# Graph attention on one core: first edges of nodes found from one gathered chunk row per group of seven nodes

## What is computed

```
h = relu(layernorm(x));  x = x + gat(h, [src, dst], edge_attr)
h = (h @ W_node.T)              # 4 heads x 32
e = (edge_attr @ W_edge.T)
att = sum([h[src], h[tgt], e] * a);  att = leaky(att, 0.2)
m = max(segment_max(att, tgt), 0);  ex = exp(att - m[tgt])
denom = segment_sum(ex, tgt) + (num_edges - deg) * exp(-m)
h_prime = segment_sum(ex / denom[tgt] * h[src], tgt)
```

## Time and profile before

| | us |
|---|---|
| median of 3 runs | 4975.68 |
| their range | 4975.63 to 4978.6 |
| profiled execution | 4962.95 |
| its span in the trace | 4955.9 |
| busy: POOL / DVE / ACT / PE | 3712.2 / 2412.0 / 1368.3 / 777.3 |

### The profile page before, as it was taken

How to read it: one execution, slowest core, us unless ns; L and a number is a source line. 1 busy time by engine, 2 the same in 40 slices (tenths; PEclk the granted TensorE clock), 3 DMA queues, 4 the chain that set the end, 5 groups by cost and what they waited for, 6 DMA issues and landing times.

```text
span 4955.9 us, 14358 instructions
## 1 busy us (share of the span) xinstructions
PE 777.3 (16%) x1453; PEld 390.6 (8%) x1453; DVE 2412.0 (49%) x2384; ACT 1368.3 (28%) x1021; POOL 3712.2 (75%) x3530
## 2 busy tenths in 40 slices
PE   5321111111111111111111111111111111111100
PEld 3310000000000000000000000000000000000000
DVE  7337454545445454454544545445454454544543
ACT  7013232222322222222222322223222232222320
POOL 6667777777777777777777777777777777777766
PEclk9555555555555555555555555555555555555555
DMA  7234444343443434434344343433434434343353
GB/s 250 90 132 119 140 123 128 114 137 114 126 125 114 137 114 128 123 115 137 114 127 123 114 136 114 129 121 115 137 114 128 122 115 136 114 131 120 116 170 104
DMA packets 171831, 627.97 MB, mean 127 GB/s; under 512 B 72897, under 2 KB 73666, under 8 KB 155426
## 3 DMA queue, kind: packets, MB, share of 16 engines
q0 software_dynamic: 115936, 252.37, 21.0%
q1 hardware_dynamic: 55874, 375.39, 20.1%
HBM read 382.66 MB, written 244.86 MB: 127 GB/s over the span
## 4 chain that ended last, share of the span: by engine, by line
POOL 70%; issue 24%; another core or an unknown queue 2%; ACT 2%; DVE 1%; PE 0%; DMA 0%; POOLq 0%; ACTq 0%; DVEq 0%; SPq 0%
POOL slots L308 69%; ACT pen L375 1%; DVE pen L482 0%; PE ae L792 0%; DVE slots L496 0%; ACT big L392 0%; ACT slots L391 0%; POOL tdst_scratch L311 0%; ACT R L421 0%; PE wexp L785 0%; DMA state_scratch<-R 0%; DVE V L636 0%; DVE slots L501 0%; DMA cols<-in_cols_dram 0%
## 5 line engine op out<-in xcount | busy, mean ns | idle before, releaser
L308 POOL DMA_INDIRECT slots<-rows_scratch,idx x3224 | 3421.5, 1061 | 1066.5 <-issue 1066.5
L803 PE MATMUL ae<-eab,w_att 128*128 128x416 f32 x992 | 650.6, 829 | 3796.2 <-DMA eab<-in_ea_dram 2539.1
L603 DVE TENSOR_TENSOR z<-slots,big 128x104 f32<-128x104 f32 (+1 forms) x125 | 43.1, 345 | 2116.3 <-DMA slots<-rows_scratch,idx 1887.3
L636 DVE TENSOR_TENSOR_SCAN V<-A,V 128x1848 f32<-128x1848 f32 x248 | 993.7, 4007 | 35.4 <-issue 4.8
L421 ACT COPY R<-V 128x1716 f32<-128x1716 f32 x248 | 777.8, 3136 | 339.1 <-DVE V L636 196.7
L417 ACT ACTIVATE A<-D 128x1848 f32<-128x1848 f32 x246 | 419.7, 1706 | 744.7 <-DVE V L636 410.3
L803 PEld LDWEIGHTS ae<-eab,w_att 128*128 128x128 f32 x992 | 296.0, 313 | 4150.4 <-issue 3384.4
L626 DVE TENSOR_TENSOR V<-slots,wexp 128x1716 f32<-128x1716 f32 x125 | 404.8, 3239 | 22.4 <-issue 21.0
L626 DVE TENSOR_TENSOR V<-slots,extra 128x1716 f32<-128x1716 f32 x123 | 398.2, 3237 | 22.0 <-issue 16.3
L438 ACT ACTIVATE wexp<-D 128x104 f32<-128x104 f32 x62 | 16.2, 261 | 1092.5 <-DVEq L621 628.8
L438 ACT ACTIVATE extra<-D 128x104 f32<-128x104 f32 x61 | 15.9, 261 | 1063.2 <-DVEq L621 631.2
(11 more groups left out here) (168 smaller groups left out, 602.3 us busy)
## 6 DMA issues: line engine op xcount, KB each, us to landing
state_scratch<-R SPq DMA_DIRECT2D x123, 1768.0 KB
eab<-in_ea_dram SPq DMA_DIRECT2D x126, 832.0 KB
slots<-rows_scratch,idx POOLq DMA_INDIRECT x3224
rows_scratch<-slots SPq DMA_DIRECT2D x14, 476.0 KB
tdst_scratch<-eab SPq DMA_DIRECT2D x4, 1612.0 KB
big<-tdst_scratch SPq DMA_DIRECT2D x8, 806.0 KB
big<-in_x_t_dram SPq DMA_DIRECT2D x14, 448.0 KB, 4.3
big<-in_x_dram SPq DMA_DIRECT2D x7, 896.0 KB
```

Of the source, the lines that this page charges most:

```text
L308: pool.indirect_dma_start(buf, None, table, bass.IndirectOffsetOnAxis(ap=index, axis=0)).then_inc(done, 16)
L636: nc.vector.tensor_tensor_scan(V[:, v, :], a_all, V[:, v, :], 0.0, ALU.mult, ALU.add).then_inc(scanned, 1)
L803: last = mm(ps_ae[k][:, 0:KB * Q], w_att[:, a * P:(a + 1) * P], eab[:, k, a * KB * Q:(a + 1) * KB * Q], start=a == 0, stop=a == 3)
```

## The change

The list is now cut into `CL` = 1024 chunks of `CE` = 403 edges. Only the first node of each group of seven has its chunk looked up (14 counts on ACT over 1024 values, 14 gathers, all into buffers of their own). All seven nodes of the group are counted in that one row: groups 2, 3, 6, 7, 8, 11, 12 and 13 (`BY_ACT`) by ACT with a Sign over 403 values, the other six by DVE. One node more, the first of the next group, is counted early by DVE where a batch ends.

A node whose first edge lies beyond that chunk gets it in another way. For each chunk (eight on a partition) and each of the six nodes that follow the last target of the chunk before, DVE counts the values below the node in the chunk (`chunk_heads`, 48 counts over 403 values of `dst_s`). The results are scattered in eight scatters as rows of six to `heads_scratch`, which is filled with a large negative number beforehand, and loaded back; `latest_heads` takes for each node the maximum of what the chunk heads up to six nodes before it say, and `positions` the maximum of that and the count. The positions are made in three batches of groups, 0 to 3, 4 to 8 and 9 to 13.

The load of `dst` moves ahead of the 14 loads of `x_t`. The making of `pen_a` (before: lines 540 to 543) moves behind the last projection copy. SP gets the fill of `heads_scratch`, their load behind the fills of `tdst_scratch`, and a small DMA that brings each partition the count of the next one's first node.

```diff
-CL = 512
-CE = P * T // CL
+CHUNKS = 8
+CL = P * CHUNKS
+CE = T // CHUNKS
...
-COUNTS = (0, 2, 4, 7, 12, 20, 29, 38, 47, 56, 65, 74, 83, 92, 99)
+FOLLOW = NG - 1
+LOOKED_UP = (0, 2, 4, 7, 10, 14)
+BATCHES = ((0, 4), (4, 9), (9, 14))
+BY_ACT = (2, 3, 6, 7, 8, 11, 12, 13)
...
+            sp.dma_start(heads_d[0:NP, :].rearrange("(p w) j -> p (w j)", p=P), fill[:, 0:W * FOLLOW]).then_inc(heads_filled, 16)
             for k in range(H):
                 sp.wait_ge(centre_done, 8 + k)
                 sp.dma_start(td_rows[:, k * T:(k + 1) * T], fill).then_inc(tdst_filled, 16)
+            sp.wait_ge(heads_put, 16 * CHUNKS)
+            sp.dma_start(heads, heads_d[0:NP, :].rearrange("(p w) j -> p (w j)", p=P)).then_inc(heads_loaded, 16)
+            sp.wait_ge(put_ready, 1)
+            sp.dma_start(cnt[0:P - 1, W:W + 1], cnt[1:P, 0:1]).then_inc(next_count, 16)
...
-            for k in range(W + 1):
-                if k in COUNTS:
-                    pool.wait_ge(chunk_ready, COUNTS.index(k) + 1)
-                if k >= RING:
-                    pool.wait_ge(chunk_used, k - RING + 1)
-                gather(ring[:, k % RING, :], dst16[:, :], chunk_i[:, k:k + 1], chunk_dma[k % RING])
+            for g in range(STEPS):
+                if g in LOOKED_UP:
+                    pool.wait_ge(chunk_ready, LOOKED_UP.index(g) + 1)
+                gather(ring[:, g, :], dst16[:, :], chunk_i[:, g:g + 1], chunk_dma[g])
+            pool.wait_ge(heads_filled, 16)
+            pool.wait_ge(heads_ready, 1)
+            for c in range(CHUNKS):
+                scatter(heads_d[:, :], head_i[:, c:c + 1], head_pos[:, c * FOLLOW:(c + 1) * FOLLOW], heads_put)
             pool.wait_ge(tdst_filled, 64)
             for g in range(STEPS):
-                pool.wait_ge(put_ready, 1 if g < STEPS - 1 else 2)
+                pool.wait_ge(put_ready, sum(g >= a for a, b in BATCHES))
...
+            def count_group(g):
+                act.wait_ge(chunk_dma[g], 16)
+                for n in range(NG):
+                    k = g * NG + n
+                    nc.scalar.activation(junk_c[n], ring[:, g, :], ACT.Sign, bias=half_n[:, k:k + 1], scale=-1.0, accum_out=sgn_w[:, k:k + 1])
+                act.drain()
+                nc.scalar.activation(within[:, g * NG:(g + 1) * NG], sgn_w[:, g * NG:(g + 1) * NG], ACT.Copy, bias=CE / 2.0, scale=0.5).then_inc(act_counted, 1)
...
+            def chunk_heads():
...
+                for j in range(FOLLOW):
+                    dve.drain()
+                    for c in range(CHUNKS):
+                        k = c * FOLLOW + j
+                        nc.vector.tensor_scalar(junk_v[c], dst_s[:, c * CE:(c + 1) * CE], bound[:, k:k + 1], None, ALU.is_lt, ALU.add,
+                                                accum_out=below[:, k:k + 1])
...
+            def latest_heads():
...
+                dve.wait_ge(heads_loaded, 16)
+                for j in range(1, NG):
+                    nc.vector.tensor_tensor(to[:, :, j:NG], to[:, :, j:NG], of[:, :, 1:NG + 1 - j, j - 1], ALU.max)
+                    dve.drain()
...
+                dve.wait_ge(act_counted, sum(g < gb for g in BY_ACT))
...
+                nc.vector.tensor_tensor(cnt[:, a:b], cnt[:, a:b], head_max[:, a:b], ALU.max)
...
+            chunk_heads()
+            count_groups(0, 4, True)
+            variance(0)
+            variance(1)
+            latest_heads()
+            inverse_deviation()
+            positions(0)
+            for g in range(3):
+                project_copy(g)
+            count_groups(4, 9, True)
+            project_copy(3)
+            dve.drain()
+            positions(1)
+            project_copy(4)
+            project_copy(5)
+            count_groups(9, 14, False)
+            project_copy(6)
+            dve.drain()
+            positions(2)
             nc.vector.tensor_scalar(rest[:, :], deg[:, :], -1.0, float(E), ALU.mult, ALU.add).then_inc(rest_ready, 1)
-            for g in range(2, STEPS):
+            for g in range(7, STEPS):
                 project_copy(g)
+            nc.vector.tensor_tensor(pen_a[:, 1:T], dst_s[:, 1:T], dst_s[:, 0:T - 1], ALU.is_equal)
+            nc.vector.memset(pen_a[:, 0:1], 0.0)
+            dve.drain()
+            nc.vector.tensor_scalar(pen_a[:, :], pen_a[:, :], 2.0 * BIG, -BIG, ALU.mult, ALU.add).then_inc(pen_a_done, 1)
```

More of the change, by code:

```diff
@@ L3 @@
 from contextlib import ExitStack
+import itertools
 P = 128
@@ L32, with graph_attention_kernel @@
 ITERS = PAIRS // UP
-RING = 8
 PIECES = 8
 PT = T // PIECES
-COUNTS = (0, 2, 4, 7, 12, 20, 29, 38, 47, 56, 65, 74, 83, 92, 99)
+FOLLOW = NG - 1
+LOOKED_UP = (0, 2, 4, 7, 10, 14)
+BATCHES = ((0, 4), (4, 9), (9, 14))
+BY_ACT = (2, 3, 6, 7, 8, 11, 12, 13)
 Q = 32
 GW = P + Q
-def graph_attention_kernel(nc, x, x_t, src, dstf, dst16, lasts, ends, first, ea, w_node, w_node_t, a_blk, we2,
+def graph_attention_kernel(nc, x, x_t, src, dstf, dst16, lasts, chunk_ends, ends, first, ea, w_node, w_node_t, a_blk, we2,
                            ident_c, centre_c, cols_c, out):
@@ L372, in count_chunks @@
             def count_chunks(m):
-                a, b = COUNTS[m], COUNTS[m + 1]
-                for k in range(a, b):
-                    nc.scalar.activation(junk_a[k % 9], last_b[:, :], ACT.Sign, bias=half_n[:, k:k + 1], scale=-1.0, accum_out=sgn[:, k:k + 1])
+                a, b = LOOKED_UP[m], LOOKED_UP[m + 1]
+                for g in range(a, b):
+                    nc.scalar.activation(junk_a[g % 4], last_b[:, :], ACT.Sign, bias=half_n[:, g * NG:g * NG + 1], scale=-1.0, accum_out=sgn[:, g:g + 1])
                 act.drain()
@@ new lines, in count_groups @@
+            def count_groups(a, b, after_last):
+                for g in range(a, b):
+                    if g not in BY_ACT:
+                        dve.drain()
+                        for n in range(g in starts, NG):
+                            count_within(g * NG + n)
+                if after_last:
+                    starts.append(b)
+                    count_within(b * NG, NG)
+            def chunk_heads():
+                prev, last = chunk_s[:, 0:CHUNKS], chunk_s[:, CHUNKS:2 * CHUNKS]
+                base, spare = cols[:, W + 4:W + 4 + CHUNKS], cols[:, W + 4 + CHUNKS:W + 4 + 2 * CHUNKS]
+                by_j = lambda t: t.rearrange("p (c j) -> p c j", j=FOLLOW)
+                dve.wait_ge(loaded_lasts, 32)
+                dve.wait_ge(loaded_chunks, 16)
+                for j in range(FOLLOW):
+                    nc.vector.tensor_scalar(by_j(bound)[:, :, j], prev, float(j + 1), None, ALU.add)
+                nc.vector.tensor_tensor(head_ok, last, prev, ALU.is_gt)
+                nc.vector.scalar_tensor_tensor(head_n, prev, 1.0, spare, ALU.add, ALU.subtract)
+                dve.drain()
+                nc.vector.tensor_tensor(head_n, head_n, head_ok, ALU.mult)
+                dve.drain()
+                nc.vector.tensor_tensor(head_i[:, :], head_n, spare, ALU.add)
+                dve.wait_ge(loaded_dst, 16)
+                for j in range(FOLLOW):
+                    dve.drain()
[4 more added lines that the diff above has]
+                dve.drain()
+                nc.vector.tensor_tensor(by_j(head_pos), by_j(below), base.rearrange("p (c j) -> p c j", j=1).broadcast_to([P, CHUNKS, FOLLOW]),
+                                        ALU.add).then_inc(heads_ready, 1)
@@ L530, in inverse_deviation @@
                 dve.drain()
-            EARLY = W - NG
-            dve.wait_ge(loaded_lasts, 32)
-            for k in range(W + 1):
-                if k % RING == 0:
-                    dve.drain()
-                count_within(k)
-                if k == 60:
-                    dve.wait_ge(loaded_dst, 16)
-                    nc.vector.tensor_tensor(pen_a[:, 1:T], dst_s[:, 1:T], dst_s[:, 0:T - 1], ALU.is_equal)
-                    nc.vector.memset(pen_a[:, 0:1], 0.0)
-                    dve.drain()
-                    nc.vector.tensor_scalar(pen_a[:, :], pen_a[:, :], 2.0 * BIG, -BIG, ALU.mult, ALU.add).then_inc(pen_a_done, 1)
-                if k == 72:
-                    variance(0)
-                if k == 80:
-                    variance(1)
-                if k == 84:
-                    inverse_deviation()
-                if k == 88:
-                    project_copy(0)
-                if k == EARLY:
-                    dve.drain()
-                    positions(0, EARLY, 0)
-                if k == EARLY + 4:
-                    project_copy(1)
@@ L557, in _ @@
-            dve.drain()
-            positions(EARLY, W, EARLY + 1)
+            starts = []
+            nc.vector.memset(head_max, -BIG)
+            nc.vector.memset(cnt[:, W:W + 1], float(E))
+            chunk_heads()
[8 more added lines that the diff above has]
+            count_groups(4, 9, True)
```

89 lines of the change are left out of this document (62 added, 27 removed).

## The result

The changed kernel takes **4890.46 us** (median of 4 runs, 4889.39 to 4892.25) against 4977.14 (4975.63 to 4981.23) for the kernel before in the same runs: ratio 0.9825, 95% interval 0.9808 to 0.9842, 86.7 us faster. The forecast was 4932.5 with a range from 4903 to 4961: right in sign, half the size, and the range did not hold it. (Before's median was 4975.68 when the forecast was made; a fourth run moved it to 4977.14.)

A forecast was written before the change was run, and what follows sets the result against it. POOL was taken to bound all stages, with the node chain setting the first scatter. First scatter -52.6, a pause +6.4 and pen_a +3 gave -43.2 us: execution 4962.95 to 4919.8, median 4932.5, range 4903 to 4961.

The forecast's parts named there:

- The loop stays: Edge loop: the change leaves it alone, so its 4490 us stay unchanged.
- each microsecond at 305.75 is a microsecond of the kernel: First loop gather, at 305.75 us before: each microsecond it comes earlier shortens the kernel, unless something else is late.
- 14 gathers and 8 scatters on POOL under cover: POOL before 60 us: the 8 head scatters' 10 us cost nothing, since POOL would be idle.
- The chain without excess, V = 81.3 us: Node chain (centre, square, variance) up to V, its last variance: 3 slow and 11 fast steps take 81.3 us.
- Excess, +14.5: Node chain: unexplained delay, 30 us in the old chain, taken as 14.5 for one half as long; V = 96.
- rival 1: Node chain runs without excess: V = 81, kernel 4918 us; chance 0.17.
- V to first scatter, 12.5: From the last variance to the first scatter: 12.5 us instead of 18.0, so first scatter at 108.5.
- A fourth pause, +6.4: Scatter stage: one more POOL pause of 6.4 us, from late row stores with two buffers; four in all.
- Rival 3: Scatter stage: a pause at every pair of groups, seven in all, 19 us more, 4952 us; chance 0.12.
- pen_a, +3: Edge comparison moved beside the last scatters: holds up POOL there, 3 us on the path, bounds 0 and 4.5.
- whole 4.5 us: pen_a's two steps on DVE: by the skill's port rule all 4.5 us would be lost, 1.5 us more.
- The offset of 12.7 from execution to median: Whole kernel: the median lies 12.7 us above the profiled execution, so 4919.8 becomes 4932.5.

The follow-up runs named there:

- e8: Kernel after with 79 counts over 512 values put back between ACT's node steps, without look-ups (same kernel as e3, another chip): 4934.35 us.
- e9: Kernel after with 36 useless gathers of 31 numbers on POOL beside the node chain (same kernel as e1, another chip): 4927.47 us.
- e10: Kernel before without ACT's 79 counts between node steps, part of the computation left out (same kernel as e2, another chip): 5019.14 us.
- e6: e5 with five row buffers for the projected rows instead of two: 4888.36 us, 0.9832 of before.
- e7: Kernel after with two memsets on POOL ahead of its 17th scatter, as a break in its transfers: 4897.91 us, 0.9863 of before.
- e12: e11 with pen_a made ahead of the variance instead of behind the last copy: 4890.23 us.
- b1: Kernel before, unchanged, traced again on another chip: 4970.93 us.
- fourth group: Last set of runs, on one chip: the kernel after, e11 and e12, beside before at 4968.14 us.
- quick chip: Chip of the first group of runs (e1 to e4), where the kernel before takes 4464.72 us.
- e5: Kernel after with DVE's counts and first positions ahead of the variance, early root table load, ACT's counts behind the deviations: 4888.87 us, 0.9838 of before.
- a1: Kernel after, unchanged, run again in the second group: 4886.78 us, 0.9836 of before.
- e11: e5 with DVE's copies of node groups 4 to 13 in two loops instead of written out: 4884.63 us, 0.9833 of before.
- e1: Kernel after with 36 useless gathers of 31 numbers on POOL beside the node chain: 4414.05 us.
- e3: Kernel after with 79 counts over 512 values put back into ACT's first nine node steps, without look-ups: 4455.48 us.
- e2: Kernel before without ACT's 79 counts between node steps, part of the computation left out: 4550.72 us.
- e4: Kernel after with five row buffers for the projected rows instead of two: 4408.94 us, 0.9876 of before.

## Why the prediction was wrong

In the order of its steps:

- **The loop stays**: right, 4490.52 against 4490.3. So was "each microsecond at 305.75 is a microsecond of the kernel": loop 71.8 earlier, span 71.0 shorter.
- **14 gathers and 8 scatters on POOL under cover**: right; the last head scatter ends at 50.5, and POOL then waits 38.96.
- **The chain without excess, V = 81.3 us**: 76.4 measured. The first variance matmuls came at 25.76 instead of 27.5 (1.7), the three steps at the lower clock level, as said, took 18.0 instead of 18.6, and those at the upper mostly 3.07 instead of 3.2. The sum also counted 11 whole steps at the upper level, and the last has only its variance matmuls (1.72).
- **Excess, +14.5: the step that failed.** Measured 0. I had scaled an unexplained delay with the length of the chain. The delay itself was about as large as I took it for the old chain (30 us; 24 to 33 by e8), but e8, e9 and e10 show that it goes with transfers in a row on POOL beside the chain, and the change takes 85 of 99 of them away. The rows shown before held the hint: ACT's 9.62 us stop ended at 135.11, 2.8 us after POOL's last gather before its wait of 12.18 us. I gave this case 0.17 (rival 1, V = 81); its mechanism came true, though its time, 4918, was 27.5 us too long.
- **V to first scatter, 12.5**: 13.1.
- **A fourth pause, +6.4**: also wrong. There are three, 16.5 us together against 19.2 before, so -2.7 in place of +6.4, 9.1 us off. I took them for waits on row stores; e6 refutes that, and e7 shows what ended one of them. Rival 3 rested on the same reading.
- **pen_a, +3**: 2.55 (3.52 against 0.97); e12 confirms the cause. The Trainium skill, SBUF — State Buffer, "Who interferes with whom", says of VectorE's two-port modes that whichever engine issues first has the shared port pair for the whole instruction and the other one blocks fully. Of an instruction with two SBUF inputs, such as the comparison, it says that it contends with a GpSimd instruction that reads SBUF. The traces agree with a full block under both passes: the held scatter ended 0.12 us after the second. The "whole 4.5 us" of the prediction is the upper bound: a scatter that is under way runs on, so less is lost.
- **The offset of 12.7 from execution to median**: the third error, 14.5 us, as after's median is 1.8 below its execution. I carried it over as a constant. It was probably more of the same stops: b1's execution with V 9.0 later is 8.0 longer, and on the chip of the fourth group nine runs of before spread over 17.9 us, five of after over 6.5. That the offset came from the chain is not shown, since only two chains of before were traced, on different chips.

By terms, for the first loop gather: -43.2 was forecast; V came 19.6 earlier than forecast, the way to the first scatter was 0.6 longer, pauses cost 9.1 and pen_a 0.5 less. That gives -71.8. The rest of after's execution took 1.1 us longer, so the two executions differ by 70.7. The medians add 14.2 and 1.8, which makes 86.7. On the quick chip the change is worth less: with five row buffers 55.8 us.

## What to carry to other kernels

An unexplained wait must not be scaled with the stretch in which it stands. List for each such wait what every other engine did when it began and when it ended. Here most of the stops that POOL then waited for ended 2.4 to 5.5 us behind the end of a row of indirect transfers, and that would have told which way the term goes. And when a change removes the part of a program that varies from run to run, do not carry the baseline's offset over as it is.

Moving work ahead to start a limited stream sooner (e5) brings nothing if the stream then waits longer for its supply; read the pauses before counting on the start.

## What the runs showed of the hardware

- Beside an uninterrupted row of indirect transfers on GpSimd, ScalarE, VectorE and TensorE stopped, ScalarE for up to 23 us (e10). In the three traces of after the pauses stand at the same scatters; in the two of before the stops of the chain and the pauses do not. The engines went on 2.4 to 5.7 us after the row had ended, or in the midst of it. 36 gathers of 62 bytes a partition were enough (V 116.79 against 78.46 on the same chip); 14 gathers and 8 scatters were not (after, e8).
- An indirect transfer that GpSimd starts while VectorE compares two inputs in SBUF (3.51 us) is held until 0.11 to 0.12 us after VectorE's next pass (1.00 us; before, after, a1, e11). One that is under way takes its usual 0.95 to 0.97 us (before, after).
- A kernel on the quick chip and the same on another: V 69.67 and 116.79 (e1, e9), 113.95 and 119.22 (e3, e8), the chain of e2 and e10 63.67 and 123.76. On the quick chip no trace had such a stop in its chain or a pause in its scatters. There the loop's gathers take 947 ns with 0.305 us between them, against 1061 ns and 0.331 us, which is 450 us of the whole. The group of loop gathers in e4, as the earlier trace rows:

```profile
L331 POOL DMA_INDIRECT slots<-rows_scratch,idx x3224 | 3053.7, 947 | 982.6 <-issue 982.6
```

- Whether the stops and the slower gathers have one cause is not known. I had not expected chips to differ so much for the same program: what gains 1.7% on one gains 1.2% on the other (there with five row buffers, which change nothing in e6 against e5).
